# Expert layer by single 128-row tiles: ten versions with announced jumps, and a ring of twelve weight slots filled from the second attention on

## The chip, the cores and the metric

One Trainium2 chip, eight cores. Every core runs the same program on its own sequence of 2048 tokens; all eight read the same weights from memory. The metric is the device time of the slowest core, in microseconds (us). TensorE multiplies matrices, ScalarE applies functions, VectorE works element by element, GpSimd issues the transfers that convert float32 weights to bfloat16 as they load, SyncE issues the others. Results of TensorE go to eight PSUM banks of 128 x 512 float32.

## The reference

Two transformer layers on x of 8 x 2048 x 1024. Layer 0: causal attention with 16 heads, then a dense feed-forward part with ternary weights. Layer 1: attention whose queries, keys and values are projected to rank 32 per head, then eight experts of which each token uses two:

```python
logits = xf @ router_w.T
scores = jax.nn.softmax(logits, axis=-1)
topk_scores, topk_ids = jax.lax.top_k(scores, 2)
topk_scores = topk_scores / topk_scores.sum(-1, keepdims=True)
cw = (one_hot(topk_ids, 8) * topk_scores[..., None]).sum(1)
for wg, wu, wd, w in experts:            # 1024 x 4096, 1024 x 4096, 4096 x 1024
    h = silu(xf @ wg) * (xf @ wu)
    acc = acc + w[:, None] * (h @ wd)
```

Each part works on the layer norm of x and is added to x.

## The kernel before

The program is a row of blocks with a barrier between them: layer norm, projections, attention and output projection of layer 0; its feed-forward part; then in layer 1 `fold_low_rank` (which multiplies the projection weights by the low-rank matrices), `layernorm` with eight buffers of tokens, `low_rank_projections`, `attention` and `out_proj_residual`; then `moe` with `route`, `experts`, `overflow` and `combine`. In the second attention SyncE writes zeros to the result array `ye` and GpSimd only fills one row of zeros.

`route` sends each token's normed row to two of the 8 x 2048 rows of `xg` and writes to `ntile` how many tiles of 128 rows each expert has (`nt`). Every core has its own counts.

`experts` handles the experts one after the other. The counts are known only at run time, so each engine's instructions hold several versions of the work and jump to the one that fits. For expert e:

- TensorE turns token tiles around (`transposes`, group g of four tiles), ScalarE copies them to `xT` (`evacuate`). Group 0 of the next expert is done at the end of this expert's gate and up, group 1 between the two down halves, group 2 (the ninth tile) after the second. SyncE loads them from `xg` into `xs`, which holds two groups.
- `gate_up`: 32 steps `fc`, each of 128 of the 4096 inner features. A step takes the rows of the expert in column blocks of at most 512, given by `GU_BLOCKS`, and for each block 8 matmuls for gate and 8 for up. ScalarE applies silu to gate (`gates`), VectorE multiplies by up into `h` (`ups`). Three pairs of PSUM banks take turns. The version is chosen by `by_tiles`, nested If and Else whose bodies lie in a row: five-step version, four, three, two, one, none. Its columns are 256, 512, 768, 1024 or 1152, for up to 2, 4, 6, 8 and 9 tiles.
- `down`: two halves `dh` of 512 output columns. Each tile takes 32 matmuls of 512 columns (`while_tiles`: nested Ifs, one per tile), VectorE casts it to `y`, SyncE stores it to `ye`. Before the gate matmuls of the next expert TensorE waits for VectorE's mark `yall`.
- Weights go through a ring of five slots of 16 KB per partition (2 MB in bfloat16), 12 per expert: gate and up in turn by 1024 features, then four of down. GpSimd loads slot s once TensorE has counted slot s - 5 as read (`rel`), and the first five as the block begins. Gate and up pieces are 2 KB long in SBUF, down pieces 1 KB.

`overflow` handles more than nine tiles and is skipped when no expert has them. `combine` gathers the two result rows of each token and adds them to x.

Of the kernel before, what the change touches and what calls it, by code (L numbers as in the profile page):

```python
# [8 lines left out]
F32 = mybir.dt.float32  # L9
# [238 lines left out]
def attention(k, q, kk, v, y, P, causal, scale, zero, weights=()):  # L248
# [34 lines left out]
    with k.sbuf("at_p", [128, nr * 1536], BF16) as p, k.sbuf("at_raw", [128, 1024], F32) as raw, \  # L283
# [371 lines left out]
def fold_low_rank(k, W, wqz, wkz, wvz, woz, bqk, bvz, bo):  # L655
# [152 lines left out]
def l1_attention(k, x_in, x_out, W, ye):  # L808
    with contextlib.ExitStack() as es:
# [3 lines left out]
        with contextlib.ExitStack() as ws:  # L813
            tb = lambda name, n, p=128, dt=BF16: ws.enter_context(k.sbuf(name, [p, n], dt))
            wqz, wkz, wvz = tb("b_wqz", DC * 512), tb("b_wkz", DC * 512), tb("b_wvz", DC * 512)
            bqk, bvz = tb("b_bqk", 8, 128, F32), tb("b_bvz", 512, 1)
            fold_low_rank(k, W, wqz, wkz, wvz, woz, bqk, bvz, bo)
            xln = tb("b_xln", DC * T)
            layernorm(k, x_in, xln)
            low_rank_projections(k, xln, wqz, wkz, wvz, bqk, bvz, zq, zk, zv)  # L820
        attention(k, zq, zk, zv, y, 4, False, float(R) ** -0.5, ye)
# [3 lines left out]
def route(k, x_in, W, xg, pidx, cwt, ntile):  # L825
# [8 lines left out]
    with contextlib.ExitStack() as es:  # L834
# [177 lines left out]
        def _(s):  # L1012
# [9 lines left out]
            for tc in range(KC + 2):  # L1022
# [17 lines left out]
def by_tiles(eng, nt, emit):  # L1040

    with eng.If(nt > 4):
        with eng.If(nt > 8):
            emit(5)
        with eng.Else():
            with eng.If(nt > 6):
                emit(4)
            with eng.Else():
                emit(3)
    with eng.Else():  # L1050
        with eng.If(nt > 2):
            emit(2)
        with eng.Else():
            with eng.If(nt > 0):
                emit(1)
            with eng.Else():
                emit(0)
# [10 lines left out]
def experts(k, W, xg, ye, ntile):  # L1068
# [7 lines left out]
    with contextlib.ExitStack() as es:  # L1076
        sb = lambda name, shape, dt: es.enter_context(k.sbuf(name, shape, dt))
        ring = sb("ex_ring", [128, RING * 8192], BF16)
# [7 lines left out]

        def slot(s):
            return ring[:, (s % RING) * 8192:(s % RING) * 8192 + 8192]

# [10 lines left out]
        def _(g):  # L1100
            counts("gpsimd", g)
            for e in range(NE):
                for i in range(12):
                    s = 12 * e + i
                    if s >= RING:
                        g.wait_ge(rel, s - RING + 1)
                    if i < 8:
                        j, up = divmod(i, 2)
                        src = W["w_up" if up else "w_gate"][e].rearrange("(c p) n -> p c n", p=128)[:, :, j * 1024:j * 1024 + 1024]
                        g.dma_start(out=slot(s).rearrange("p (c n) -> p c n", c=DC), in_=src).then_inc(wl[s % RING], 16)  # L1110
                    else:
                        dh, hh = divmod(i - 8, 2)
                        src = W["w_down"][e].rearrange("(c p) n -> p c n", p=128)[:, hh * 16:hh * 16 + 16, dh * 512:dh * 512 + 512]
# [430 lines left out]
```

## Time and profile before

| | |
|---|---|
| median of 3 runs | 4458.08 us (4457.49 to 4468.6) |
| profiled execution | 4485.97 us, span of its slowest core (core 1) 4484.4 us |
| TensorE (matmuls) busy | 3478.2 us, 78% of the span |
| ScalarE busy | 1357.1 us, 30% |
| VectorE busy | 1071.7 us, 24% |
| weights through GpSimd's queue | 234.92 MB written, 31.6% of 16 engines |

Core 1 is in the expert stage from about 2472 to 4394 us, in `route` before it and in `combine` after it. The profile's rows are told by engine and line: L1191 are the gate and up matmuls, L1215 the down matmuls, L1165 the transposes of tokens, L1248 ScalarE's copies of these, L1258 silu, L1288 the product by up, L1302 the cast of a result tile. An idle time stands before an instruction with what ended it; "issue" means that the engine waited for nothing that the profile shows.

### The profile page before, as it was taken

The page shows a single profiled execution, that of the slowest core. Times are in us where ns is not written, and L with a number is a line of the kernel's source. Part 1 is how long each engine was busy: PE and PEld are TensorE (multiplying, and loading weights), DVE is VectorE, ACT ScalarE, POOL GpSimd, SP SyncE. Part 2 cuts the span into 40 slices and gives each one's busy share as a digit, 9 for nine tenths or more (in the row PEclk, how much of TensorE's full clock was granted, in tenths as well). Part 3 has the DMA queues.
Part 4 walks back from the last instruction along what each step waited for, and adds up shares of the span by engine and source line. Part 5 has one row for each costly group of instructions (what it writes and reads, how often), then busy time and mean ns, then how long its engine had stood idle before and what let it go on. Part 6 is the DMA issues. An engine that isn't in the chain of part 4 may idle for free. (4 is left out here: it accounts for less than half of the span.)

```text
span 4484.4 us, 50106 instructions; the slowest of 8 cores (4318.8 to 4484.4 us)
## 1 busy us (share of the span) xinstructions
PE 3478.2 (78%) x19308; PEld 1630.1 (36%) x19308; DVE 1071.7 (24%) x1519; ACT 1357.1 (30%) x1456; POOL 178.3 (4%) x199
## 2 busy tenths in 40 slices
PE   3988883249999477776762999898988989899871
PEld 2433331134444232111252554343433644344350
DVE  3245543690000341111230111111110211111013
ACT  2157641342111027999431111121110211112010
POOL 0000000000000000000003000000000000000003
PEclk9999996559999679999955999999999999999985
DMA  6073028771111627100335858997444558844496
GB/s 131 1 214 106 1 61 284 237 244 29 38 38 38 85 76 257 45 1 1 123 103 136 129 89 149 153 158 138 75 80 89 87 88 165 153 72 73 80 170 232
DMA packets 253791, 496.59 MB, mean 111 GB/s; under 512 B 25088, under 2 KB 99840, under 8 KB 249344
## 3 DMA queue, kind: packets, MB, share of 16 engines
q0 software_dynamic: 149552, 234.92, 31.6%
q1 hardware_dynamic: 103888, 256.98, 17.8%
q8 instruction: 222, 3.64, 0.3%
q14 instruction: 129, 1.06, 0.1%
HBM read 591.50 MB, written 118.49 MB: 158 GB/s over the span
## 5 line engine op out<-in xcount | busy, mean ns | idle before, releaser
L1191 PE MATMUL ps<-ex_xT,ex_ring 128*128 128x512 bf16 (+1 forms) x6144 | 1190.4, 358 | 92.7 <-issue 66.4
L1191 PEld LDWEIGHTS ps<-ex_xT,ex_ring 128*128 128x128 bf16 x6144 | 608.4, 99 | 675.1 <-issue 121.8
L349 ACT ACTIVATE at_p<-ps 128x1536 bf16<-128x1536 f32 (+3 forms) x542 | 724.6, 1496 | 128.7 <-PE ps L311 126.0
L1215 PE MATMUL ps<-ex_ring,ex_h 128*128 128x512 bf16 x2304 | 522.9, 391 | 71.9 <-issue 64.4
L1288 DVE TENSOR_TENSOR ex_h<-ps,ex_h 128x512 bf16<-128x512 f32 (+1 forms) x384 | 239.9, 625 | 1117.8 <-ACT ex_h L1258 1117.8
L1258 ACT ACTIVATE ex_h<-ps 128x512 bf16<-128x512 f32 (+1 forms) x384 | 208.6, 544 | 937.2 <-PE ps L1191 937.1
L1215 PEld LDWEIGHTS ps<-ex_ring,ex_h 128*128 128x128 bf16 x2304 | 229.9, 100 | 361.9 <-issue 106.9
L329 PE MATMUL ps<-at_p,onesb 128*32 128x512 bf16 (+4 forms) x1664 | 298.5, 383 | 0.0
L311 PE MATMUL ps<-b_zq,b_zk 32*128 32x512 bf16 x1024 | 139.3, 395 | 121.8 <-ACT at_p L349 120.5
L608 PE MATMUL ps<-f_xln,f_w1t 128*128 128x512 bf16 x1024 | 223.1, 381 | 6.3 <-DMA f_b<-L_ffn_b 6.3
L620 PE MATMUL ps<-f_w2t,f_h 128*128 128x512 bf16 x1024 | 226.5, 379 | 0.0
L1302 DVE CAST ex_y<-ps 128x512 bf16<-128x512 f32 x72 | 49.8, 692 | 601.2 <-PE ps L1215 588.7
L633 ACT ACTIVATE f_h<-ps,f_b 128x512 bf16<-128x512 f32 x128 | 87.8, 687 | 306.8 <-PE ps L608 306.8
L1258 ACT ACT_TABLE_LOAD x8 | 10.3, 1283 | 549.0 <-PE ps L1191 549.0
L329 PE MATMUL ps<-at_p,a_v 128*64 128x512 bf16 (+3 forms) x640 | 135.2, 380 | 41.9 <-DVE at_raw L368 41.6
L370 DVE RECIPROCAL at_inv<-at_raw 128x512 f32<-128x512 f32 x48 | 160.9, 3353 | 5.0
L329 PE MATMUL ps<-at_p,b_zv 128*32 128x512 bf16 x1024 | 144.0, 402 | 20.6 <-DVE at_raw L368 16.1
L183 PE MATMUL ps<-identb,ln_xn 128*128 128x128 bf16 x384 | 47.9, 306 | 130.8 <-DVE ln_xn L162 126.3
L367 DVE COPY at_raw<-ps 128x512 f32<-128x512 f32 x48 | 33.2, 692 | 482.4 <-PE ps L329 481.6
L608 PEld LDWEIGHTS ps<-f_xln,f_w1t 128*128 128x128 bf16 x1024 | 100.2, 98 | 128.2 <-issue 9.1
L311 PEld LDWEIGHTS ps<-b_zq,b_zk 32*128 32x128 bf16 x1024 | 42.0, 91 | 287.1 <-issue 287.1
L620 PEld LDWEIGHTS ps<-f_w2t,f_h 128*128 128x128 bf16 x1024 | 97.9, 98 | 120.6 <-issue 6.3
(200 smaller groups left out, 2480.1 us busy)
## 6 DMA issues: line engine op xcount, KB each, us to landing
ex_ring<-L_ffn_w_gate POOLq DMA_DIRECT2D x32, 2048.0 KB, 27.5
ex_ring<-L_ffn_w_up POOLq DMA_DIRECT2D x32, 2048.0 KB, 15.8
ex_ring<-L_ffn_w_down POOLq DMA_DIRECT2D x32, 2048.0 KB, 22.8
xg<-at_zrow SPq DMA_DIRECT2D x16, 2048.0 KB, 22.6
th_w<-L_ffn_W SPq DMA_DIRECT2D x32, 1024.0 KB, 9.9
te_w<-L_ffn_W SPq DMA_DIRECT2D x64, 512.0 KB, 5.0
ye<-at_zrow SPq DMA_DIRECT2D x16, 2048.0 KB, 22.6
ln_x<-x SPq DMA_DIRECT2D x48, 512.0 KB, 6.7
```

The lines of the kernel that those rows point to most:

```text
L311: m = pe.matmul(k.psum[:, (n % 2) * 1536 + o:(n % 2) * 1536 + o + 512 - 128 * d], kk[j * w:j * w + w, g * T + kc * 128:g * T + kc * 128 + ...
L329: m = pe.matmul(k.bank(bank)[j * w:j * w + w, 128 * d:512], lhs, p[:, (n % nr) * 1536 + o:(n % nr) * 1536 + o + 512 - 128 * d], start=(i, ...
L349: s.activation(p[:, (n % nr) * 1536:(n % nr) * 1536 + width[n]], k.psum[:, (n % 2) * 1536:(n % 2) * 1536 + width[n]], AF.Exp, scale=scale) ...
L370: vec.reciprocal(inv[:, :], raw[:, 512:1024]).then_inc(rc, 1)
L608: m = pe.matmul(k.bank(i % 4), w1t[:, dc * FF + fc * 128:dc * FF + fc * 128 + 128], xln[:, dc * T + c * 512:dc * T + c * 512 + 512], start ...
L620: pe.matmul(k.bank(b), h[:, fc * 512 + tt * 128:fc * 512 + tt * 128 + 128], w2t[:, fc * D + hf * 512:fc * D + hf * 512 + 512], start=fc == ...
L633: s.activation(h[:, fc * 512:fc * 512 + 512], k.bank(i % 4), AF.Gelu, bias=b1[:, fc:fc + 1]).then_inc(ge, 1)
L1191: m = pe.matmul(k.bank(2 * (i % 3) + half, w), slot(s)[:, dc * 1024 + f * 128:dc * 1024 + f * 128 + 128], xT[:, dc * CAP + o:dc * CAP + o ...
L1215: m = pe.matmul(k.bank(3 * dh + t % 3), h[:, fc * CAP + t * 128:fc * CAP + t * 128 + 128], slot(s0 + fc // 16)[:, (fc % 16) * 512:(fc % 16 ...
L1258: s.activation(h[:, fc * CAP + o:fc * CAP + o + w], k.bank(2 * (i % 3), w), AF.Silu).then_inc(sil[e], 1)
L1288: v.tensor_mul(ht, k.bank(2 * (i % 3) + 1, w), ht).then_inc(hdn[e], 1)
L1302: v.tensor_copy(y[:, o:o + 512], k.bank(3 * dh + t % 3)).then_inc(yv[dh][e], 1)
```

## The change

Gate and up get a version for each count of tiles from 0 to 9, with as many columns as the tiles have. The blocks are of at most 512 columns, often 384. `by_tiles` is written out with labels: a tree of compares, then for every version its first step, then for every version the other 31 steps. The jumps from a first step to its rest and from a rest to the end are announced: at the start of the part a branch hint names where its last jump goes. The entry jumps of the tree are not announced.

The ring has twelve slots of 8 KB per partition (1 MB), 24 per expert; gate and up slots hold 512 features in pieces of 1 KB. It is allocated for the whole of layer 1. The folded weights and the normed tokens of the second attention lie in it until the projections are done; its layer norm has six buffers in place of eight. In the attention's block GpSimd then issues the loads of the first twelve slots; in `experts` it goes on from the thirteenth. `xs` holds one group of four tiles in place of two, so a load of group 1 or 2 waits until the group before it has been transposed. ScalarE's block ends with a drain under a condition that holds only when `overflow` has work.

```diff
+            if prefetch is not None:
+                prefetch(g)
...
-        raw = [sb(f"fo_w{i}", DC * D) for i in range(3)]
-        wo, wot = sb("fo_wo", DC * D), sb("fo_wot", DC * D)
+        wo, wot, *raw = [spare[:, i * DC * D:(i + 1) * DC * D] for i in range(4)]
+        raw.append(sb("fo_w2", DC * D))
...
+        bqk, bvz = sb("b_bqk", 8, 128, F32), sb("b_bvz", 512, 1)
+        wqz, wkz, wvz = [ring[:, i * DC * 512:(i + 1) * DC * 512] for i in range(3)]
+        xln = ring[:, 3 * DC * 512:3 * DC * 512 + DC * T]
+        fold_low_rank(k, W, wqz, wkz, wvz, woz, bqk, bvz, bo, ring[:, 3 * DC * 512:])
+        layernorm(k, x_in, xln, nb=6)
+        low_rank_projections(k, xln, wqz, wkz, wvz, bqk, bvz, zq, zk, zv)
+        attention(k, zq, zk, zv, y, 4, False, float(R) ** -0.5, ye, prefetch=prefetch)
...
-GU_BLOCKS = {0: (), 1: ((0, 256),), 2: ((0, 512),), 3: ((0, 512), (512, 256)), 4: ((0, 512), (512, 512)),
-             5: ((0, 512), (512, 512), (1024, 128))}
-RING = 5
...
+GU_BLOCKS = {0: (), 1: ((0, 128),), 2: ((0, 256),), 3: ((0, 384),), 4: ((0, 512),),
+             5: ((0, 384), (384, 256)), 6: ((0, 384), (384, 384)), 7: ((0, 512), (512, 384)), 8: ((0, 512), (512, 512)),
+             9: ((0, 384), (384, 384), (768, 384))}
+RING, SLOT = 12, 4096
+GU_SLOTS, SLOTS = 16, 24
+
+
+def by_tiles(k, eng, nt, first, rest):
+
+
+    nc = k.nc
+    k.nbuf += 1
+    label = lambda part, v="": f"tiles{k.nbuf}_{part}{v}"
+
+    def choose(lo, hi):
+        if lo == hi:
+            eng.br(label("first", lo))
+            return
+        mid = (lo + hi) // 2
+        eng.br_cond(nt > mid, label("over", f"{mid}_{hi}"), label("upto", f"{lo}_{mid}"))
+        nc.enter_bb(label("over", f"{mid}_{hi}"))
+        choose(mid + 1, hi)
+        nc.enter_bb(label("upto", f"{lo}_{mid}"))
+        choose(lo, mid)
+
+    choose(0, CT)
+    for v in range(CT + 1):
+        nc.enter_bb(label("first", v))
+        ahead = eng.mark_branch_hint_location()
+        first(v)
+        eng.br(label("rest", v)).branch_hint(ahead)
+    for v in range(CT + 1):
+        nc.enter_bb(label("rest", v))
+        ahead = eng.mark_branch_hint_location()
+        rest(v)
+        eng.br(label("end")).branch_hint(ahead)
+    nc.enter_bb(label("end"))
+
+
+def weight_slot(ring, s):
+    return ring[:, (s % RING) * SLOT:(s % RING) * SLOT + SLOT]
+
+
+def load_slot(k, g, W, ring, s):
+
+
+    e, i = divmod(s, SLOTS)
+    if i < GU_SLOTS:
+        j, up = divmod(i, 2)
+        src = W["w_up" if up else "w_gate"][e].rearrange("(c p) n -> p c n", p=128)[:, :, j * 512:j * 512 + 512]
+    else:
+        dh, a = divmod(i - GU_SLOTS, 4)
+        src = W["w_down"][e].rearrange("(c p) n -> p c n", p=128)[:, a * 8:a * 8 + 8, dh * 512:dh * 512 + 512]
+    g.dma_start(out=weight_slot(ring, s).rearrange("p (c n) -> p c n", c=8), in_=src).then_inc(k.ring[s % RING], 16)
...
-        xs = sb("ex_xs", [128, 2 * 4 * D], BF16)
+        xs = sb("ex_xs", [128, 4 * D], BF16)
...
+            for s in range(RING, SLOTS * NE):
+                g.wait_ge(rel, s - RING + 1)
+                load_slot(k, g, W, ring, s)
...
+                q.dma_start(out=xs[:, 0:n * D].rearrange("p (a n) -> p a n", a=n),
...
                     with q.If(nt[e + 1] > 4):
+                        q.wait_ge(xtr[e + 1], 4)
                         load(e + 1, 1)
...
+            def landed(s):
+                pe.wait_ge(wl[s % RING], 16 * (s // RING + 1))
+
...
+                def block(vn, f, b):
+                    o, w = GU_BLOCKS[vn][b]
+                    sg = SLOTS * e + 2 * (f // 4)
+                    i = f * len(GU_BLOCKS[vn]) + b
+                    if i >= 3:
+                        pe.wait_ge(hdn[e], i - 2)
+                    for half, s in ((0, sg), (1, sg + 1)):
+                        for dc in range(DC):
+                            m = pe.matmul(k.bank(2 * (i % 3) + half, w),
+                                          weight_slot(ring, s)[:, dc * 512 + f % 4 * 128:dc * 512 + f % 4 * 128 + 128],
+                                          xT[:, dc * CAP + o:dc * CAP + o + w], start=dc == 0, stop=dc == DC - 1)
+                            if f > 0 and f % 4 == 0 and b == 0 and half == 0 and dc == 0:
+                                m.then_inc(rel, 2)
+                    m.then_inc(gum[e], 1)
+
+                def first(vn):
+                    pe.wait_ge(xev[e], min(CT, 4 * max(1, (vn + 3) // 4)))
                     if e >= 1:
                         pe.wait_ge(yall, e)
-                    for j in range(4):
-                        sg, su = 12 * e + 2 * j, 12 * e + 2 * j + 1
-                        pe.wait_ge(wl[sg % RING], 16 * (sg // RING + 1))
-                        pe.wait_ge(wl[su % RING], 16 * (su // RING + 1))
-                        if not vn:
-                            if j < 3:
+                    landed(SLOTS * e)
+                    landed(SLOTS * e + 1)
+                    for b in range(len(GU_BLOCKS[vn])):
+                        block(vn, 0, b)
+
+                def rest(vn):
+                    for f in range(1, FC):
+                        if f % 4 == 0:
+                            landed(SLOTS * e + f // 2)
+                            landed(SLOTS * e + f // 2 + 1)
+                            if not vn:
                                 pe.drain().then_inc(rel, 2)
-                            continue
-                        for f in range(8):
...
+                        for b in range(len(GU_BLOCKS[vn])):
+                            block(vn, f, b)
...
+                        pe.wait_ge(hdn[e], 32 * len(GU_BLOCKS[vn]))
+
+                by_tiles(k, pe, nt[e], first, rest)
 
             def down(e, dh):
-                s0 = 12 * e + 8 + 2 * dh
-                for s in (s0, s0 + 1):
-                    pe.wait_ge(wl[s % RING], 16 * (s // RING + 1))
+                s0 = SLOTS * e + GU_SLOTS + 4 * dh
+                for a in range(4):
+                    landed(s0 + a)
...
-                pe.drain().then_inc(rel, 2)
+                pe.drain().then_inc(rel, 4)
...
+                by_tiles(k, s, nt[e], lambda vn: part(vn, range(1)), lambda vn: part(vn, range(1, FC)))
...
+        with k.sbuf("m_ring", [128, RING * SLOT], BF16) as ring:
+            def prefetch(g):
+                for s in range(RING):
+                    load_slot(k, g, Wf, ring, s)
+
+            l1_attention(k, x_in, x_mid, Wa, ye, ring, prefetch)
+            route(k, x_mid, Wf, xg, pidx, cwt, ntile)
+            tiles = experts(k, Wf, xg, ye, ntile, ring)
```

## Rows read from the trace of the kernel before

**Rows 1.** Spans and granted clock of cores 1, 2 and 7.

```profile
core 1: 4484.4 us, clock 0.876
core 2: 4458.9 us, clock 0.877
core 7: 4447.7 us, clock 0.876
```

**Rows 2.** Core 2 by expert: result casts, clock, DMA share, GB/s.

```profile
2452.80:2642.10 189.30, 5.53 (x8) 0.95 0.95 152
2642.10:2821.90 179.80, 4.15 (x6) 0.94 0.92 151
2821.90:3000.10 178.20, 4.15 (x6) 0.95 0.94 159
3000.10:3424.90 424.80, 12.45 (x18) 0.95 0.40 75
3424.90:3689.30 264.40, 6.92 (x10) 0.95 0.55 99
3689.30:3871.30 182.00, 4.15 (x6) 0.94 0.93 157
3871.30:4240.60 369.30, 11.07 (x16) 0.95 0.44 81
4240.60:4370.00 129.40, 2.77 (x4) 0.85 0.89 136
```

**Rows 3.** Core 2, TensorE's waits, 2400 to 4380: total, times, longest.

```profile
PE ps L1215 <- issue: 67.4, 15, 13.6
PE ps L1191 <- issue: 60.1, 9, 13.2
PE ps L1165 <- ACT ex_xT L1248: 36.2, 18, 9.4
```

**Rows 4.** Core 2, TensorE in order of time; idle before in brackets.

```profile
2945.04 15.22 PE L1215 MATMUL ps<-ex_ring,ex_h 128*128 128x512 bf16 x62 [6.01 <-issue]
...
3000.07 1.86 PE L1191 MATMUL ps<-ex_xT,ex_ring 128*128 128x512 bf16 x4 [2.86 <-ACT ex_xT L1248]
...
3263.05 1.93 PE L1165 MATMUL ps<-identb,ex_xs 128*128 128x128 bf16 x16 [9.41 <-ACT ex_xT L1248]
3278.49 64.09 PE L1215 MATMUL ps<-ex_ring,ex_h 128*128 128x512 bf16 x282 [13.52 <-issue]
3424.91 1.91 PE L1191 MATMUL ps<-ex_xT,ex_ring 128*128 128x512 bf16 x4 [13.22 <-issue]
...
4240.56 1.65 PE L1191 MATMUL ps<-ex_xT,ex_ring 128*128 128x256 bf16 x7 [12.02 <-issue]
```

**Rows 5.** Core 2, VectorE's products: a three-tile and a five-tile expert.

```profile
2907.10 0.69 DVE L1288 TENSOR_TENSOR ex_h<-ps,ex_h 128x512 bf16<-128x512 f32 x1 [2.76 <-ACT ex_h L1258]
2910.56 0.69 DVE L1288 TENSOR_TENSOR ex_h<-ps,ex_h 128x512 bf16<-128x512 f32 x1 [2.76 <-ACT ex_h L1258]
...
3559.41 0.69 DVE L1288 TENSOR_TENSOR ex_h<-ps,ex_h 128x512 bf16<-128x512 f32 x1 [3.24 <-ACT ex_h L1258]
3564.61 0.69 DVE L1288 TENSOR_TENSOR ex_h<-ps,ex_h 128x512 bf16<-128x512 f32 x1 [3.24 <-ACT ex_h L1258]
```

**Rows 6.** Core 2, TensorE's first gate matmuls.

```profile
2452.83 1.48 PE L1191 MATMUL ps<-ex_xT,ex_ring 128*128 128x512 bf16 x3 [23.08 <-DMA ex_ring<-L_ffn_w_up]
```

**Rows 7.** GB/s in 40 slices: core 1, gate/up, down; then core 2, window.

```profile
GB/s 37 70 164 205 188 209 205 197 209 217 221 201 205 221 213 213 205 217 217 209 205 209 213 238 197 213 209 213 213 213 213 213 213 205 221 213 213 205 217 217
...
GB/s 0 11 11 141 194 166 145 186 192 201 203 207 209 207 235 194 203 205 209 209 207 201 205 207 209 207 209 207 216 209 209 209 207 207 209 209 209 209 209 209
...
2500.00:2560.00 60.00, 59.74 (x275) 27.20 (x279) 12.46 (x18) 10.31 (x18) 4.29 (x4) 1.00 1.09 165
```

**Rows 8.** Core 1, second attention (window); core 2, loads of tokens.

```profile
1551.00:2180.00 629.00, 445.76 (x3599) 135.22 (x3601) 149.61 (x192) 493.58 (x396) 0.95 (x1) 0.92 0.21 68
...
ex_xs<-xg SPq DMA_DIRECT2D x2, 1024.0 KB, 18.9
```

More of the change, by code:

```diff
@@ L245, in _, with attention @@
                 vec.tensor_copy(target(n), k.bank(n % 4)).then_inc(evv, 1)
-def attention(k, q, kk, v, y, P, causal, scale, zero, weights=()):
+def attention(k, q, kk, v, y, P, causal, scale, zero, weights=(), prefetch=None):
     nc = k.nc
@@ L1065, in while_tiles, with experts @@
             while_tiles(eng, nt, emit, t + 1)
-def experts(k, W, xg, ye, ntile):
+def experts(k, W, xg, ye, ntile, ring):
     nc = k.nc
@@ L1101, in _ @@
             counts("gpsimd", g)
[L1102 to L1113, printed above, removed]
-                        g.dma_start(out=slot(s).rearrange("p (c n) -> p c n", c=16), in_=src).then_inc(wl[s % RING], 16)
+            for s in range(RING, SLOTS * NE):
+                g.wait_ge(rel, s - RING + 1)
+                load_slot(k, g, W, ring, s)
         @block.sync
@@ L1149, in _ @@
                         with q.If(nt[e + 1] > 8):
[L1150 removed]
+                            q.wait_ge(xtr[e + 1], 8)
                             load(e + 1, 2)
@@ L1174, in version @@
                     if e >= 1:
                         pe.wait_ge(yall, e)
-                    for j in range(4):
-                        sg, su = 12 * e + 2 * j, 12 * e + 2 * j + 1
-                        pe.wait_ge(wl[sg % RING], 16 * (sg // RING + 1))
-                        pe.wait_ge(wl[su % RING], 16 * (su // RING + 1))
-                        if not vn:
-                            if j < 3:
-                                pe.drain().then_inc(rel, 2)
-                            continue
-                        for f in range(8):
-                            for b, (o, w) in enumerate(blocks):
-                                i = (j * 8 + f) * len(blocks) + b
-                                if i >= 3:
-                                    pe.wait_ge(hdn[e], i - 2)
-                                for half, s in ((0, sg), (1, su)):
-                                    for dc in range(DC):
-                                        m = pe.matmul(k.bank(2 * (i % 3) + half, w),
-                                                      slot(s)[:, dc * 1024 + f * 128:dc * 1024 + f * 128 + 128],
-                                                      xT[:, dc * CAP + o:dc * CAP + o + w], start=dc == 0, stop=dc == DC - 1)
-                                        if j >= 1 and f == 0 and b == 0 and half == 0 and dc == 0:
-                                            m.then_inc(rel, 2)
-                                m.then_inc(gum[e], 1)
@@ L1215, in tile @@
                         m = pe.matmul(k.bank(3 * dh + t % 3), h[:, fc * CAP + t * 128:fc * CAP + t * 128 + 128],
-                                      slot(s0 + fc // 16)[:, (fc % 16) * 512:(fc % 16) * 512 + 512],
+                                      weight_slot(ring, s0 + fc // 8)[:, (fc % 8) * 512:(fc % 8) * 512 + 512],
                                       start=fc == 0, stop=fc == FC - 1)
@@ L1251, in gates, with part @@
             def gates(e):
-                def version(vn):
-                    blocks = GU_BLOCKS[vn]
-                    for fc in range(FC if vn else 0):
-                        for b, (o, w) in enumerate(blocks):
-                            i = fc * len(blocks) + b
+                def part(vn, fcs):
+                    for fc in fcs:
+                        for b, (o, w) in enumerate(GU_BLOCKS[vn]):
+                            i = fc * len(GU_BLOCKS[vn]) + b
                             s.wait_ge(gum[e], i + 1)
                             s.activation(h[:, fc * CAP + o:fc * CAP + o + w], k.bank(2 * (i % 3), w), AF.Silu).then_inc(sil[e], 1)
-                by_tiles(s, nt[e], version)
+                by_tiles(k, s, nt[e], lambda vn: part(vn, range(1)), lambda vn: part(vn, range(1, FC)))
             evacuate(0, 0)
@@ L1274, in _ @@
                             evacuate(e + 1, 2)
+            with s.If(nt[NE] > CT):
+                s.drain()
         @block.vector
@@ L1280, in ups, with part @@
             def ups(e):
-                def version(vn):
-                    blocks = GU_BLOCKS[vn]
-                    for fc in range(FC if vn else 0):
-                        for b, (o, w) in enumerate(blocks):
-                            i = fc * len(blocks) + b
+                def part(vn, fcs):
+                    for fc in fcs:
+                        for b, (o, w) in enumerate(GU_BLOCKS[vn]):
+                            i = fc * len(GU_BLOCKS[vn]) + b
                             v.wait_ge(sil[e], i + 1)
@@ L1288, in version @@
                             v.tensor_mul(ht, k.bank(2 * (i % 3) + 1, w), ht).then_inc(hdn[e], 1)
-                by_tiles(v, nt[e], version)
+                by_tiles(k, v, nt[e], lambda vn: part(vn, range(1)), lambda vn: part(vn, range(1, FC)))
             for e in range(NE):
@@ L1530, in build_program @@
     l0_ffn(k, x1, x2, part("L0_ffn_"))
-    l1_attention(k, x2, x3, part("L1_attn_"), ye)
-    moe(k, x3, out, part("L1_ffn_"), xg, ye)
+    layer1(k, x2, x3, out, part("L1_attn_"), part("L1_ffn_"), xg, ye)
     return nc, stack
```

54 lines of the change are left out of this document (8 added, 46 removed).

## The prediction

> **What bounds the kernel now.** I read the cores' spans first [rows 1]: core 1 ends last, core 2 is 25 us behind it in length, and their two dies are alike. Then the windows of core 2, one per expert [rows 2]. Each token tile gives two result casts, so the counts 8, 6, 6, 18, 10, 6, 16, 4 say 4, 3, 3, 9, 5, 3, 8 and 2 tiles of 128 rows: 37 in all. The same view of core 1 gives 5, 3, 3, 8, 5, 3, 7, 2 (36), of core 7 it gives 4, 3, 3, 9, 5, 3, 8, 1. The experts take 1917 us of core 2's 4459, the change rewrites that stage, and so I sum on it.
>
> TensorE is the main limit there, at a mean granted clock of 0.94 or 0.95. But the DMA column is the one to watch: the three-tile experts already draw on it for 92 to 94% of their time at 151 to 159 GB/s, the long ones for 40 to 44%. Time taken from a three-tile expert soon meets the weights; time taken from a long one does not.
>
> Third, the waits [rows 3] and the places where they fall [rows 4]. On core 2, 67 us before down matmuls and 60 us before gate and up matmuls end in nothing but "issue": no semaphore was late. They follow the layout of the code. Leaving a three-tile version means jumping over one body (6.01 us idle), leaving a nine-tile one means two jumps (13.52); entering the nine-tile version, which lies next, has none (its 2.86 us are ScalarE's copy), entering the five-tile one from behind two bodies has 13.22, the last expert's 12.02. I read some 6 us per far jump, the time to fetch instructions. The Trainium skill (Runtime: NRT & Kernel Launch, section on instruction fetch mechanics) says that a taken branch outside the resident pages waits for a fetch by DMA; the rows agree. By it alone the ten versions keep their stalls, and the sum below would lack the terms for leaving and entering.
>
> **The change, part by part, on core 2.**
>
> *Columns.* Before, gate and up ran in steps of 256 columns, so 3, 5 and 7 tiles were padded by 128. One step of the five-tile version takes 5.20 us (3559.41 to 3564.61), of the 512-column one 3.46 (2907.10 to 2910.56) [rows 5]; 256 columns cost 1.74 us, 128 cost 0.87, over 32 steps 27.8 us. Core 2 has four such experts (3, 3, 5, 3): **-111 us**. Nine tiles go from 512+512+128 to three times 384, the same columns: 0. If weights pace an expert instead, its part of the 111 is not had; that is taken below.
>
> *Leaving a version.* The jump to the end is announced as the rest begins, tens of microseconds ahead. Seven exits idle 6 to 7 us (five of them) or 13.5 (two), together 60 of the 67.4 us; I leave 0.5 us each: **-57**. No row shows an announced jump, so the bounds are 0 and -60; I take the far end because the notice is so long. ScalarE leaves its version the same way, and once TensorE waited 9.41 us for it where the other 17 waits average 1.6: **-8**.
>
> *Entering.* A tree of compares and then the first step of each version, close together. Of the 60.1 us, 44.5 lie before experts 1 to 6 (the 12.0 and a second stall of 3.5 before the last one count below). Five of those entries have an idle. VectorE's last cast and mark must still come, skipped result tiles must be passed, and the first step of a narrow version (2.6 us at 384 columns) may be too short to hide the second jump. I leave 4.5 us each, between the 1.5 us that the mark needs and the 8.9 of now: **-22**, bounds 0 and -37.
>
> *First expert.* Its weights come during the attention, so the 23.08 us that TensorE idles after its transposes [rows 6] shrink to ScalarE's last copy and one jump, about 5: **-18**. On cores whose first expert has five tiles the single xs buffer gives some of that back: the second load waits for the first four transposes.
>
> *Twelve transfers more in the attention.* GpSimd issues them and has nothing else to do then. In that stretch ScalarE is busy 494 of 629 us and DMA 21% [rows 8]: 12 MB hide. Uncovered they would cost 12 times 6.4 = 77 us, as they did in part before. Layer norm with six buffers, moved tiles in SBUF and seven more semaphores neither remove nor add a wait that I can name: 0, within the 10 us added below.
>
> *Smaller transfers, deeper ring.* A slot is 1 MB in 1 KB pieces. Down slots had this form already: once running they stream mostly at 201 to 209 GB/s, gate and up slots with their 2 KB pieces mostly at 205 to 217 [rows 7]. When all cores load, it is 165 GB/s (core 2, 2500 to 2560). So a slot takes 6.4 us, and 5.1 alone. GpSimd's issue of the next lies beside that.
>
> *Where the weights now pace it.* At the start of expert 1 eight of its slots are in (the last four only come free as the expert before ends). By the start of the second down half of expert 2, 40 more must land, with 3 MB of tokens (half the memory reads of a weight byte, so 3.2 us each) and some results: 257 + 10 + 3 = 270 us. TensorE's own work up to there is two three-tile experts of 138 us (83 gate and up; 41 down, from nine tiles in 64.09 us [rows 4]; 5 transposes; 9 jumps and starts at low clock), less the last down half of 21: 255 us. **+15**, bounds 0 (alone, 5.1 us a slot) and +42 (7.1 us). Expert 5, also of three tiles, stands between five and eight tiles: 16 slots, 103 us, against 117: no wait.
>
> *Last expert.* Now 141 us from the end of the eight-tile down to its last cast (129.4 [rows 2] and 12.0 idle ahead [rows 4]). It starts with eight slots in; 16 more need 103 us, then 14 us for the last down half and 2 of latency: 119. **-22**. It stays bound by weights, so neither its columns nor its entry jump count.
>
> *The xs buffer.* The load of tiles 4 to 7 of the next expert goes out as the down half begins and lands in some 18.9 us [rows 8]; a three-tile half takes 23. Hidden, by 4 us; if it comes late, twice a few us. Behind it on SyncE's queue stand the stores of results, which VectorE needs only from its third tile on.
>
> *Sum.* 111 + 57 + 8 + 22 + 18 + 22 - 15 = 223: core 2 goes from 4459 to 4236. Core 1, by the same steps: six padded experts 167, exits 55, ScalarE 8, entries 19, start 13, last expert 16, less 15: 263, to 4221. Core 7: 221, to 4227. So core 2 becomes the slowest. The profiled execution took 4486 us for a span of 4484.4, and the median of the runs is 4458, 28 below it. 4236 + 2 - 28 gives 4210. I add 10 for the ends of the sum, most of which (announced jumps, weights) lie on the slow side: **4220 us**.
>
> **Rivals.**
>
> *Weights pace all small experts.* For: the 92 to 94% above [rows 2], and eight cores loading at once. Were the three 3-tile experts held at their present 178 us instead of 138, 120 us less the 15 already counted are lost: 4325. Against: the deeper ring carries slots over from long experts, which use 40% of the DMA. At 7.1 us a slot it is 27 us more at expert 2 and 11 at the last: 4258. I give 4260 to 4340 a chance of 0.18.
>
> *Announced jumps bring nothing.* Exits and ScalarE's wait stay (65 us), entries too (22): 4220 + 87 = 4307. For: no row shows such a jump, and every far jump of now stalls [rows 3, 4]. The section of the Trainium skill's page named above (Runtime: NRT & Kernel Launch) speaks for this rival too, since it knows no announcement. Against: the target is named tens of microseconds ahead, and a fetch takes 6. Chance 0.08.
>
> *Better than the sum.* Slots at 5.1 us (-15 and -20), entries at the mark (-15), and less work at the low clock: a mean of 0.94 over 178 us is 21 us at 1.2 GHz, mostly idle; what falls on matmuls costs some 4 us an expert (up to -30). About 4150 with most of it. Chance 0.1.
>
> *Slower.* A gate or up slot now reads 2 KB pieces 16 KB apart, where a down slot's lie 4 KB apart. If each small piece cost as much as the large one did, the expert stage would be a queue of transfers: 116 gate and up slots at x and 64 down slots at 6.4 us, with 50 us for tokens and results and 14 for the last tiles, reach today's 1935 us when x passes 12.6 us. At 12.9 (twice the present time per byte) it is 1971: 4495. Against: the small pieces stream as fast as the large ones [rows 7]. Chance 0.04.
>
> **How the numbers follow.** The forecast, 4220 with its own range of 4185 to 4260, has 0.6. The range of 8 in 10 takes in the better case's nearer half and the rivals of weights and jumps: 4165 to 4325. A measurement of this kernel tells about 0.3% (13 us) from no change; every case but the slow one, and a mixture of the first two rivals at their worst, lies far under that: faster 0.94, same 0.02, slower 0.04.
>
> **What would show it.** Per expert windows of core 2 near 178, 139, 153, 391, 223, 142, 348 us and a last one of 117. Three- and five-tile steps at 2.6 and 4.3 us. "Issue" waits before down matmuls under 15 us in all. First gate matmul within 6 us of the last transpose. Waits for ex_ring only in expert 2 and the last, DMA near 165 GB/s there. The first rival would show as ring waits in experts 1, 2 and 5; the second as 6 and 13 us idles where they are now; the slow one as slots that land more than 12 us apart. The prediction is wrong first if slots take over 7 us.

## The result, and the profile after

The changed kernel takes 4324.8 us (median of four, 4313.0 to 4342.5), the kernel before beside it 4462.8: a ratio of 0.969 [0.966, 0.973]. It is faster by 3%, where 4220 us, over 5%, was forecast; the measured time lies at the upper end of the stated range of 4165 to 4325. Some executions of each kernel ran at a lower granted clock and are left out; where no ratio stands below, too few remain, and single ones are compared.

The profiled execution took 4324.97 us. Its cores' spans, beside [rows 1]:

```profile
core 1: 4238.1 us, clock 0.880
core 2: 4323.5 us, clock 0.881
```

Core 2 ends last in this execution, as forecast, but at 4323.5 us instead of 4236. In the other three it took 4271.1, 4341.0 and 4299.0 us, and in two of them core 3 ended last (4311.5 us, level with core 4, and 4323.1). Core 2's experts one by one, beside [rows 2] (length, TensorE's busy time with its instructions, granted clock, DMA share, GB/s):

```profile
2430.00:2613.50 183.50, 169.41 (x784) 0.97 0.83 127
2613.50:2772.20 158.70, 135.07 (x733) 0.91 1.13 163
2772.20:2957.50 185.30, 142.71 (x773) 0.88 1.06 162
2957.50:3356.50 399.00, 383.45 (x2165) 0.98 0.44 75
3356.50:3583.20 226.70, 214.85 (x1369) 0.98 0.78 123
3583.20:3754.60 171.40, 135.49 (x764) 0.90 1.12 164
3754.60:4109.00 354.40, 337.56 (x1536) 0.98 0.49 81
4109.00:4235.00 126.00, 93.00 (x636) 0.88 0.93 139
```

Long experts are within 8 us of the forecast (178, 391, 223, 348). The three-tile ones are 20, 32 and 29 us over their 139, 153 and 142, and the second of them is longer than before. Those are the windows with a DMA share above 1 and a clock near 0.9, where the kernel before had 0.94 or 0.95.

TensorE's waits on core 2, 2400 to 4380, beside [rows 3]:

```profile
PE ps L1201 <- issue: 59.3, 12, 8.6
...
PE ps L1244 <- DMA m_ring<-L_ffn_w_down: 43.0, 4, 14.1
PE ps L1184 <- ACT ex_xT L1277: 33.9, 17, 7.5
PE ps L1201 <- DMA m_ring<-L_ffn_w_up: 20.3, 4, 8.5
PE ps L1244 <- issue: 11.2, 12, 4.1
```

L1201 are the gate and up matmuls, L1244 down, L1184 the transposes. "Issue" before down fell from 67.4 us to 11.2: the stalls at the exits are gone. Before gate and up it stayed, 59.3 us for 60.1, and ScalarE's late copies stayed too, 33.9 for 36.2. The waits for the ring are now 63 us. The kernel before had some as well:

```profile
PE ps L1191 <- DMA ex_ring<-L_ffn_w_up: 37.7, 3, 23.1
...
PE ps L1215 <- DMA ex_ring<-L_ffn_w_down: 15.0, 2, 9.4
```

Of these 52.7 us, 23.1 are the first gate matmul's and 29.7 the last expert's. Now the first gate matmul waits for no weights, the last expert waits 23.9 us for them, and 25.2 us in expert 2 and 14.1 in expert 5 are new.

The same in order of time, beside [rows 4] and [rows 6]: the start, then experts 1 and 2.

```profile
2429.98 4.74 PE L1201 MATMUL ps<-ex_xT,m_ring 128*128 128x512 bf16 x15 [1.86 <-ACT ex_xT L1277]
...
2613.49 4.47 PE L1201 MATMUL ps<-ex_xT,m_ring 128*128 128x384 bf16 x16 [5.38 <-issue]
2622.15 83.26 PE L1201 MATMUL ps<-ex_xT,m_ring 128*128 128x384 bf16 x496 [4.19 <-issue]
2713.79 1.93 PE L1184 MATMUL ps<-identb,ex_xs 128*128 128x128 bf16 x16 [7.49 <-ACT ex_xT L1277]
...
2772.18 5.28 PE L1201 MATMUL ps<-ex_xT,m_ring 128*128 128x384 bf16 x16 [7.28 <-issue]
...
2850.53 13.21 PE L1201 MATMUL ps<-ex_xT,m_ring 128*128 128x384 bf16 x64 [6.04 <-DMA m_ring<-L_ffn_w_up]
2872.25 12.60 PE L1201 MATMUL ps<-ex_xT,m_ring 128*128 128x384 bf16 x64 [8.51 <-DMA m_ring<-L_ffn_w_up]
...
2899.14 22.94 PE L1244 MATMUL ps<-m_ring,ex_h 128*128 128x512 bf16 x94 [9.70 <-DMA m_ring<-L_ffn_w_down]
```

An entry has two stalls: one before the first step (5.38), one before the rest (4.19), whose jump was announced only as the first step began. Then, in expert 2, come four waits for the ring, the three long ones shown. At the entries of experts 4, 5 and 7, each behind a long one, the first stall is only VectorE's mark (2.2 to 2.4 us); the second is still 4.0 to 5.7 us.

VectorE's products of a three-tile expert, beside [rows 5]: a step takes 2.60 us, as forecast.

```profile
2690.50 0.56 DVE L1317 TENSOR_TENSOR ex_h<-ps,ex_h 128x384 bf16<-128x384 f32 x1 [2.04 <-ACT ex_h L1286]
2693.10 0.56 DVE L1317 TENSOR_TENSOR ex_h<-ps,ex_h 128x384 bf16<-128x384 f32 x1 [2.04 <-ACT ex_h L1286]
```

### The profile page after: what moved, and what is told of

It reads as the page before. It is cut to its first block and busy times, and to the rows that moved or that the text cites. A ratio compares the mean times of both kernels' runs of the same rounds, so it can differ in the third digit from the quotient of the medians.

```text
span 4323.5 us, 50433 instructions; the slowest of 8 cores (4172.4 to 4323.5 us)
## 1 busy us (share of the span) xinstructions
PE 3334.6 (77%) x19186; PEld 1632.2 (38%) x19348; DVE 1051.8 (24%) x1521; ACT 1346.6 (31%) x1461; POOL 255.3 (6%) x295
## 5 line engine op out<-in xcount | busy, mean ns | idle before, releaser
L1201 PE MATMUL ps<-ex_xT,m_ring 128*128 128x384 bf16 (+2 forms) x6112 | 1058.0, 336 | 94.8 <-issue 59.3
L1201 PEld LDWEIGHTS ps<-ex_xT,m_ring 128*128 128x128 bf16 x6144 | 609.5, 99 | 543.6 <-issue 130.4
L1244 PE MATMUL ps<-m_ring,ex_h 128*128 128x512 bf16 x2314 | 526.6, 388 | 56.2 <-DMA m_ring<-L_ffn_w_down 43.0
L1317 DVE TENSOR_TENSOR ex_h<-ps,ex_h 128x384 bf16<-128x384 f32 (+2 forms) x384 | 218.2, 569 | 1000.7 <-ACT ex_h L1286 1000.7
L1286 ACT ACTIVATE ex_h<-ps 128x384 bf16<-128x384 f32 (+2 forms) x384 | 191.3, 499 | 812.0 <-PE ps L1201 811.9
L1244 PEld LDWEIGHTS ps<-m_ring,ex_h 128*128 128x128 bf16 x2368 | 235.4, 100 | 344.6 <-issue 80.7
```

Source lines behind the costliest of these rows:

```text
L1201: m = pe.matmul(k.bank(2 * (i % 3) + half, w), weight_slot(ring, s)[:, dc * 512 + f % 4 * 128:dc * 512 + f % 4 * 128 + 128], xT[:, dc * CA ...
L1244: m = pe.matmul(k.bank(3 * dh + t % 3), h[:, fc * CAP + t * 128:fc * CAP + t * 128 + 128], weight_slot(ring, s0 + fc // 8)[:, (fc % 8) * 5 ...
L1286: s.activation(h[:, fc * CAP + o:fc * CAP + o + w], k.bank(2 * (i % 3), w), AF.Silu).then_inc(sil[e], 1)
L1317: v.tensor_mul(ht, k.bank(2 * (i % 3) + 1, w), ht).then_inc(hdn[e], 1)
```

## The experiments

**The notice.** `by_tiles` announces neither the jump to the rest nor the one out.

```diff
-        ahead = eng.mark_branch_hint_location()
         first(v)
-        eng.br(label("rest", v)).branch_hint(ahead)
+        eng.br(label("rest", v))
...
-        eng.br(label("end")).branch_hint(ahead)
+        eng.br(label("end"))
```

> The changed kernel without the two branch hints of each version; the layout of the code stays. Theory A (the notice hides the fetch of a far target): on core 2 the seven exits before down matmuls idle 5 to 7 us each again, and the stalls between first step and rest grow from 4 to 7 us to 5 to 9, so the time rises by 45 to 70 us, to 4370 to 4395. Theory B (the exits became short through the new layout, the notice does nothing): within 10 us of 4325.

Measured: 4357.1 us, ratio 0.975 [0.973, 0.978]. Core 2's waits:

```profile
PE ps L1199 <- issue: 58.8, 13, 8.9
...
PE ps L1242 <- issue: 49.3, 13, 8.0
PE ps L1182 <- ACT ex_xT L1275: 48.0, 13, 8.1
PE ps L1242 <- DMA m_ring<-L_ffn_w_down: 27.3, 2, 19.5
```

Announced exits are worth 38 us of stalls before down (49.3 less 11.2) and 14 for ScalarE. The entries do not change (58.8 us for 59.3). The kernel loses 0.6% (26 us by the ratios, 32 by the medians): theory A in its mechanism, but half its price of 45 to 70 us. Against the 52 us of stalls the ring waits fall from 63 us to 29 (with 1.8 before gate and up), as TensorE comes later.

**A longer first part.** First part of four steps, so that the jump to the rest has four times the notice.

```diff
+FIRST = 4
...
-                    for b in range(len(GU_BLOCKS[vn])):
-                        block(vn, 0, b)
+                    for f in range(FIRST):
+                        for b in range(len(GU_BLOCKS[vn])):
+                            block(vn, f, b)
```

> The first part of each version holds four steps of 32 instead of one, on TensorE, ScalarE and VectorE. Theory A (the notice comes too late for a step of 2.6 us): the second stalls, 41 us over eight experts on core 2, vanish; the time falls by 15 to 30 us, since part of it comes back as waits for the ring in experts 2, 5 and the last. Theory B (small experts are paced by weights, so fetch stalls only stand in for ring waits): less than 10 us. Theory C (first parts four times as long make the entry itself a far jump): entries grow by 5 us each, 4325 to 4350.

Measured: 4334.5 us, ratio 0.970 [0.968, 0.971], the same. Issue before gate and up is 55.3 us in 8 stalls instead of 59.3 in 12: fewer and longer. The ring waits of core 2 rise from 63 us to 79 (that execution, 4349.9 us, was the longest of the four). A longer notice for the second jump brings nothing: theory B.

**A quarter of the weights.** From the thirteenth slot on only two of eight row blocks are loaded; the matmuls run on what lies in the ring. The kernel's weights are incomplete, and only its time counts.

```diff
-    g.dma_start(out=weight_slot(ring, s).rearrange("p (c n) -> p c n", c=8), in_=src)...
+    c = 8 if s < RING else 2
+    g.dma_start(out=weight_slot(ring, s).rearrange("p (c n) -> p c n", c=8)[:, 0:c, :], in_=src[:, 0:c, :])...
```

> From the thirteenth slot on only a quarter of each slot's bytes is loaded (two of eight row blocks); the rest of a slot keeps what it held, so gate, up and down work on wrong weights and nothing else changes. Theory A (weights saturate the DMA engines, which holds three-tile experts and slows instruction fetches): experts 1, 2, 5 of core 2 fall from 159, 185, 171 to 138 to 145 us, the last from 126 to 95 to 100, entries lose their 5 to 9 us; in all 90 to 115 us less, 4210 to 4235. Theory B (instruction fetches cost the same whatever the weights do): ring waits of 63 us vanish, issue waits of some 80 us stay, 4260 to 4270.

Measured: 4204.8 and 4212.4 us. Core 2's experts, then its waits:

```profile
2435.40:2617.00 181.60, 172.54 (x800) 0.97 0.24 42
2617.00:2757.90 140.90, 131.16 (x737) 0.97 0.36 60
2757.90:2909.20 151.30, 135.38 (x777) 0.96 0.38 66
2909.20:3303.50 394.30, 383.19 (x2176) 0.98 0.14 28
3303.50:3529.30 225.80, 215.77 (x1377) 0.98 0.23 40
3529.30:3674.60 145.30, 134.09 (x768) 0.96 0.39 68
3674.60:4021.30 346.70, 338.88 (x1569) 0.98 0.15 27
4021.30:4115.20 93.90, 87.42 (x640) 0.96 0.32 51
```

```profile
PE ps L1185 <- ACT ex_xT L1278: 29.1, 17, 4.2
PE ps L1202 <- issue: 28.9, 11, 5.5
PE ps L1245 <- issue: 10.7, 10, 2.8
```

This is the decisive run: theory A. With the weights out of the way the first seven experts are within 4 us of the forecast each (178, 139, 153, 391, 223, 142, 348). No ring wait is left, the low clock is gone (0.96 and more), and the idle before gate and up is halved, 28.9 us for 59.3: a jump stalls longer while the weights stream. That its fetch waits behind them on the DMA fits this, but no run here shows the fetch itself.

**Slots of 16 KB.** Six of them, so 12 transfers an expert; gate and up pieces of 2 KB, the size of before.

```diff
-RING, SLOT = 12, 4096
-GU_SLOTS, SLOTS = 16, 24
+RING, SLOT = 6, 8192
+GU_SLOTS, SLOTS = 8, 12
...
-    ...[:, :, j * 512:j * 512 + 512]
+    ...[:, :, j * 1024:j * 1024 + 1024]
```

> The ring as six slots of 16 KB (2 MB) in place of twelve of 8 KB: same bytes held, gate and up pieces of 2 KB again, half as many transfers; versions and notices stay. Theory A (piece size costs nothing, as 162 to 164 GB/s in the loaded experts says): no gain from the pieces, and coarser slots wait for more bytes at once: 4325 to 4345. Theory B (the 1 KB pieces are what makes the DMA engines fall behind in small experts): GB/s in experts 1, 2 and 5 rises from 163 to 175 or more, the time falls by 15 to 40 us.

Measured: 4293.2 us, ratio 0.960 [0.957, 0.962], 1% below the change: theory B by the time, though the rate rises only to 168 to 171 GB/s. Core 2's three-tile experts:

```profile
2613.40:2769.50 156.10, 133.94 (x736) 0.95 1.08 168
2769.50:2931.20 161.70, 135.64 (x776) 0.93 1.10 171
3560.80:3718.10 157.30, 135.18 (x769) 0.93 1.07 169
```

Ring waits on core 2 are 25.3 us instead of 63.3. What the DMA did from the start of the experts to 2899.14 us, first in the change, then here (queue, packets, MB, time of the packets as a share of sixteen engines):

```profile
q0 software_dynamic: 63404, 63.94, 96.9%
```

```profile
q0 software_dynamic: 44192, 64.36, 92.2%
```

The same megabytes, in 5% less of the engines' time. A small piece of 1 KB costs 116 ns (469 us times 16 times 96.9%, over 61 slots of 1024 pieces), a large one 211 ns (6.91 ms by the same product, less 24,550 small ones at 116, over 19,150 large ones), 9% less than two small. The first row tells more: 63.94 MB are 61 slots, 73 with the twelve filled ahead, while TensorE at 2899.14 had waited 9.70 us for slots 65 to 68. It did not wait for bytes as such.

What it waited for, the semaphores in the traces show. A slot's semaphore rises in sixteen parts, and each has its time. Of slot 68 in the change the first part landed at 2847.7, the fourteenth at 2872.7, the last two at 2896.5 and 2898.5; by then the parts of 72.5 slots had landed. The table has the time from a slot's first part to its last on core 2, as a mean over all slots and over those of expert 2, in us:

| run | all slots | expert 2 |
|---|---|---|
| before, pieces of 2 KB, five slots of 16 KB | 2.1 | 2.1 |
| the change, pieces of 1 KB, twelve of 8 KB | 13.3 | 39.1 |
| a quarter of the weights | 1.7 | 1.0 |
| six slots of 16 KB, gate and up pieces of 2 KB | 4.8 | 11.3 |
| large pieces, small slots (below) | 2.4 | 3.0 |

With gate and up pieces of 1 KB a few of the sixteen parts fall far behind the rest, and a slot counts only with its last.

**The order of the experts.** 1, 3, 2, 6, 7, 4, 5, 0, so that on core 2 tiles come as 3, 9, 3, 8, 2, 5, 3, 4.

```diff
+ORDER = (1, 3, 2, 6, 7, 4, 5, 0)
...
     e, i = divmod(s, SLOTS)
+    e = ORDER[e]
```

> The change with its experts in the order 1, 3, 2, 6, 7, 4, 5, 0, so that on core 2 the tiles come as 3, 9, 3, 8, 2, 5, 3, 4: nearly every small expert stands behind a long one, and the last one has four tiles. Theory A (the ring cannot keep up through two three-tile experts in a row, and in the last expert): the ring waits of 24 us in expert 2, 14 in expert 5 and 24 in the last one go nearly all, three-tile experts fall to 160 us or less, and the kernel takes 4270 to 4290 us. Theory B (what the three-tile experts lose is the slow fetch of instructions and ScalarE, not weights): ring waits move, but the kernel stays within 15 us of the change, 4310 to 4340 us.

> The order of the run before and the six 16 KB slots together. If the two act on one thing, the wait for weights, they add up only in part: 4265 to 4285 us. If the larger pieces helped by leaving more of the DMA to instruction fetches, they add up whole: about 40 us below the run with the order alone, 4235 to 4250 us.

Measured: 4324.2 us, ratio 0.965 [0.960, 0.971], and with 16 KB slots 4301.3, ratio 0.959 [0.955, 0.964]; neither differs from the same kernel in the old order. The first is theory B; the second is above both of its theories, so the order adds nothing to the slots. On core 2 in the first (experts 2, 7 and 5 in the new order):

```profile
2987.20:3154.40 167.20, 136.31 (x768) 0.92 1.12 165
3508.50:3661.60 153.10, 99.20 (x704) 0.83 1.13 166
3888.10:4049.00 160.90, 133.74 (x736) 0.92 1.12 164
```

The two three-tile experts win 18 and 10 us, and the two-tile one, no longer last, loses 27: its 153 us are those of 24 slots at 6.4 us, although an eight-tile expert stands ahead. Ring waits fall to 37 us; issue before gate, up and down rises from 70.5 us to 81.6.

**Large pieces, small slots.** Twelve slots, 24 transfers; a gate or up slot is four row blocks of 1024 columns, released by fours.

```diff
-        j, up = divmod(i, 2)
+        j, r = divmod(i, 4)
+        up, c = r // 2, r % 2
...
-    ...[:, :, j * 512:j * 512 + 512]
+    ...[:, 4 * c:4 * c + 4, j * 1024:j * 1024 + 1024]
```

> The change with its twelve 8 KB slots and 24 transfers per expert, but a gate or up slot holds four of the eight row blocks over 1024 columns, in 2 KB pieces, and four of them are released together. If the size of the pieces made the 42 us of the 16 KB slots, this takes 4285 to 4300 us with some 168 GB/s or more in experts 1 and 2. If the number of transfers made them (24 per expert instead of 12, each with its own issue by GpSimd and its own semaphore), this takes 4315 to 4335 us at 163 GB/s.

Measured: a single execution, 4333.8 us, so the kernel's time says little: it was set by cores 4 to 7, whose clock was 0.863 to 0.870. Cores 2 and 3, at 0.883 and 0.874, took 4283.1 and 4284.8. Core 2's three-tile experts run at the higher rates:

```profile
2608.70:2765.20 156.50, 134.37 (x736) 0.93 1.08 169
2765.20:2937.40 172.20, 142.26 (x777) 0.88 1.10 174
3558.10:3714.20 156.10, 135.11 (x768) 0.93 1.07 174
```

The 22 us of ring waits that are left all stand in the last expert. Experts 2 and 5, with 39 us of them in the change, have none: slot 68 was whole at 2853.0, for 2898.5 in the change, with as many slots of the same size. The first and the last of a slot's sixteen parts are 2.4 us apart on average. One thing this run doesn't separate: here and with the 16 KB slots TensorE frees gate and up slots by 4 MB at a time, in the change by 2 MB.

**The old columns.** Three tiles at 512, five at 512 and 256, seven at twice 512, one at 256; all else as in the change.

```diff
-GU_BLOCKS = {... 1: ((0, 128),), ... 3: ((0, 384),), ...
-             5: ((0, 384), (384, 256)), ... 7: ((0, 512), (512, 384)), ...
+GU_BLOCKS = {... 1: ((0, 256),), ... 3: ((0, 512),), ...
+             5: ((0, 512), (512, 256)), ... 7: ((0, 512), (512, 512)), ...
```

> The change with the columns of the kernel before: three tiles run at 512, five at 512 and 256, seven at 512 and 512, one at 256; jumps, ring and slots stay. The prediction put this term at 111 us on core 2 (27.8 us for each of four experts). If it is had in full, this takes 4425 to 4440 us. If weights and fetches pace the three-tile experts, the 28 us are had only in the five-tile one and partly elsewhere: 4345 to 4385 us, with fewer ring waits in experts 2 and 5 than the 24 and 14 us of the change.

Measured: 4398.6 and 4395.3 us, beside a median of 4480 for the kernel before, so 0.982 where the change has 0.969: the columns are worth 1.2%, some 54 us, as far as two executions tell (core 2 alone took 4355.4 and 4393.8). Neither range had it. Core 2's experts 1, 2, 4 and 5:

```profile
2599.90:2776.90 177.00, 160.00 (x737) 0.94 1.05 156
2776.90:2959.10 182.20, 164.18 (x777) 0.95 1.00 157
3355.60:3608.90 253.30, 242.91 (x1376) 0.98 0.70 110
3608.90:3788.10 179.20, 163.36 (x768) 0.96 1.05 160
```

Against the change that is 18, -3, 27 and 8 us: the five-tile expert gains its 28 in full, three three-tile ones together 23 of 83. TensorE's busy time does fall with the new columns, by 25, 21, 28 and 28 us; in the three-tile experts it is then idle instead.

**Versions in one piece.** First step and rest stand together; only the way out is announced.

```diff
         ahead = eng.mark_branch_hint_location()
         first(v)
-        eng.br(label("rest", v)).branch_hint(ahead)
-    for v in range(CT + 1):
-        nc.enter_bb(label("rest", v))
-        ahead = eng.mark_branch_hint_location()
         rest(v)
```

> The change with each version in one piece: first step and the other 31 stand together, so that one jump leads in and the announced one leads out. In the change core 2 idles some 41 us in second stalls between the first step and the rest. Theory A (the split costs more than it hides, for its announced jump has only 2 to 3 us): the second stalls go, the entries stay as they are, TensorE's waits for issue before gate and up fall from 59 to under 30 us, and the kernel takes 4285 to 4305 us where nothing else takes the time; ring waits may take half of it back, 4305 to 4315. Theory B (what is fetched is the same code either way, and the stall only moves into the entry): 4315 to 4335 us, entries of 8 to 13 us and no second stall.

> The six 16 KB slots with versions in one piece. There the ring waits are only 25 us on core 2, so what the jumps lose shows more. Theory A: 15 to 30 us below the 16 KB slots alone, ratio about 0.954. Theory B: the same as they, ratio 0.960.

> Twelve 8 KB slots of 2 KB pieces over half the depth, with versions in one piece. If piece size is what the 16 KB slots gained by, this equals the run before within 10 us; if larger slots matter by themselves it is 20 us or more above it.

Measured: 4322.9 us, 0.964 [0.961, 0.968], with the slots of the change; 4279.4, 0.953 [0.950, 0.957], with 16 KB slots; 4287.6, 0.957 [0.953, 0.961], with large pieces in small slots. Of the first, core 2's waits, and its entry into expert 2:

```profile
PE ps L1197 <- issue: 76.9, 10, 14.5
...
PE ps L1180 <- ACT ex_xT L1273: 25.5, 19, 2.3
```

```profile
2791.02 5.13 PE L1197 MATMUL ps<-ex_xT,m_ring 128*128 128x384 bf16 x20 [14.48 <-issue]
```

The stall did move into the entry (14.48 us in place of 7.28, 2.36 and 1.84): theory B. But ScalarE is no longer late by more than 2.3 us anywhere, where it was by 7.49: its own split version had made it so. With the slots of the change this ends in the same time; with 16 KB slots it is the fastest here that does the whole work, 1.7% under the change, 4.7% under the kernel before and 0.7% under the same slots with split versions. That last is theory A's time, but not its mechanism: issue before gate and up on core 2 rose from 55.2 us to 76.4, and where the 0.7% come from stays open. The last two runs lie within 8 us of each other, with 12 and with 24 transfers an expert. So the number and size of transfers do not matter here, and the piece does, together with the grain of release named above.

## Why the prediction was right and wrong

The direction, the core that ends last (in two executions of four), the start, the exits and the longer experts came as forecast. The size did not, and the miss is nearly one term. Of 4324.8 less 4220, 105 us, 87.5 are core 2's sum in the profiled execution (its four spans run from 4271 to 4341 us, so the sum's miss is 35 to 105); 28 are the subtraction of the profiled execution's excess, less the 10 added for the ends. The terms below stand as the forecast named them; what was not had of the columns and the entries is largely time that the term of the weights should have held.

- **Columns, -111.** Had: about 50 on core 2. The 28 us were had where TensorE sets the pace, in the five-tile expert. In the three-tile ones 60 of 83 were lost.
- **Leaving, -57.** Right. Issue before down fell by 56 us, 38 of it shown by the notice taken away; the rest is the new layout or hidden in ring waits, which stand at three of the exits. The Trainium skill's rule (Runtime: NRT & Kernel Launch, instruction fetch mechanics), that a far jump waits, holds for an unannounced one: without the notice six exits on core 2 idle 5.7 to 8.0 us. The announced ones of the change idle 0.6 us at most before the first down matmul, where no ring wait hides them. They are not free every time: one each idled 5.7 us with the 16 KB slots, 6.4 with large pieces, and 6.5 in two of the runs with versions in one piece.
- **ScalarE late, -8.** Not had, 2.3 us. Its split versions cost it a late jump of its own.
- **Entering, -22.** Not had. I took 4.5 us each, as if the load on the DMA did not matter. The issue stalls of one entry make 4 to 15 us. Without most of the weights all of them are 28.9 us, and 7.0 for the mark, for the 26 that I had left (22.5, and 3.5 in the last expert).
- **First expert, -18.** Right, and 5 us better: 23 us earlier, 2452.83 to 2429.98.
- **Where the weights now pace it, +15, and small pieces, 0.** This is the step that failed. The rate was right, 162 to 164 GB/s for a forecast 165, and so were eight slots in at expert 1 (20.97 MB from 2430 to 2613.5 are 20, with twelve ahead 32, of which expert 0 took 24). Slots over 7 us, the sign named first for being wrong, did not show. What I did with it was wrong: I counted bytes. By bytes slot 68 was in well before 2899; TensorE waited all the same, for the last two of its sixteen parts. Instead of 15 us in expert 2, and none in expert 5, ring waits are 25 and 14, and with the weights streaming each jump takes longer and the granted clock is lower. The run with a quarter of the weights prices it all: from the first gate matmul to the last cast 1804 us (2430.0 to 4233.7) less 1681 (2435.4 to 4116.0), 123 us, of which the forecast held 38 (15 here and, in the last expert, 117 less 94). The other 85 are all but the sum's whole miss; that run's span on core 2, 4203.3 us, is 5 from the forecast's 4236 less 38. Of the 123, ring waits are 63, entries 30, ScalarE and transposes 11, and TensorE's longer busy time, at a lower clock, 13; 6 are spread.
- **Small pieces** are the larger part of those ring waits. [Rows 7] had shown 201 to 209 GB/s for them against 205 to 217, and I called it the same. That is 2 to 4% alone; with all cores loading a pair of them takes 232 ns of an engine's time against 211. The mean from a slot's first part to its last grew from 2.1 us to 13.3 with them. With 2 KB pieces the 39 us of ring waits in experts 2 and 5 went to none in twelve slots and to 2 in six, and the 16 KB slots gave back 1% of the kernel.
- **Last expert, -22.** 125 us to its last cast and 2.2 idle ahead, against 141: -14. It is bound by weights, as forecast, with 24 us of ring waits on the way; 22 us are left with large pieces.
- **From the profile to the median, -28.** My mistake apart from the kernel. The 28 us were core 1's, the slowest in that execution. Core 2's 4458.9 was an ordinary one: in the nineteen other executions of the kernel before that the experiments' ratios rest on it took 4446 to 4480. A sum made on core 2 needed no such correction.

The rival "weights pace all small experts" named what happened and gave 4260 to 4340; its objection, that the ring carries slots over, failed because twelve slots are half an expert, and when slot 68 was whole the parts of four more had landed that TensorE could not use yet. "Announced jumps bring nothing" fell for exits and held for entries. The slow rival fell: the slots came at 6.4 us each, not 12.

Slots complete behind their bytes because some of their parts do. The Trainium skill (DMA: Bandwidth & Descriptors, section on why a DMA increments its semaphore by 16) says that only the full count, one part from each of sixteen engines, means that all has landed, and that these engines finish independently. The traces agree: in expert 2 of the change the last part of a slot came 39 us after its first on average, 15 us after the fourteenth.

Open: why some parts lag with pieces of 1 KB. The counts don't say which engine a part came from, so whether it is always the same ones is not shown. That the larger pieces help by leaving the slowest engine slack is a reading of 96.9% against 92.2%, and the grain of release changed with them. Piece size and order were tried; a deeper or shallower ring, and the change's pieces released by 4 MB, were not.

## What to carry to other kernels

When a change moves stages towards a shared resource that is already busy (here the DMA, at 92 to 94% of the time), run the kernel with that resource lightened (here a quarter of the weights): the difference is the bill, and it holds more than waits for data. Nearly half of it here stood as longer stalls at jumps, a late second engine and a lower clock. Do not compare bytes landed with bytes needed where many transfers are in flight: a slot counts when its last part is in, so look at the spread of its parts. And announce a jump where the notice is long, as at the exits here. Splitting a body to announce the jump into its rest gained nothing: the stall only moved.

## What the hardware showed beyond that

- Stalls at jumps follow the load of weights. The entries of core 2 idle 59.3 us in all, 8.6 in the longest single stall; with a quarter of the weights 28.9 and 5.5.
- With gate and up pieces of 1 KB the first and the last of the sixteen parts of a 1 MB load landed 13.3 us apart on average on core 2, and up to 51; with pieces of 2 KB 2.4, and up to 6.
- A 2 KB piece took 9% less of the engines' time than two of 1 KB, with all cores loading (211 ns and 232).
- The granted clock of a three-tile expert was 0.94 to 0.96 with TensorE busy for 160 to 164 of 177 to 182 us (old columns) and 0.88 to 0.91 with 135 to 143 of 159 to 185 us. With a quarter of the weights it was 0.96 or 0.97, and the same matmuls took 131 to 135 us, so part of the matmul time saved was lost again.
